# Shorter pieces for a softmax denominator, one key-shift row, and a new order of work on every engine

## The reference

```
x = x + linear_attention(group_norm(x))      # layer 0
x = x + conv(group_norm(x))                  # layer 1
```

## Time and profile before

| | |
|---|---|
| median of 3 runs | 1960.87 us (1960.73 to 1961.2) |
| time of the profiled execution | 1962.26 us |
| its span, first to last instruction | 1960.5 us |
| PE, DVE, ACT, POOL busy | 1861.5, 1632.6, 1369.6, 1311.3 us |
| DVE, ACT, POOL share of the span | 83%, 70%, 67% |
| mean granted PE clock | 0.989 |

### The profile page before, as it was taken

One profiled execution on the slowest core, in us unless ns is written; L12 is line 12 of the kernel. 1 busy time (PEld: TensorE's weight loads), 2 busy tenths in 40 slices (PEclk: granted clock), 3 DMA queues, 4 the chain that ended last, 5 costly groups with the idle time before them and its releaser, 6 DMA issues.

```text
span 1960.5 us, 51383 instructions
## 1 busy us (share of the span) xinstructions
PE 1861.5 (95%) x21521; PEld 993.2 (51%) x21521; DVE 1632.6 (83%) x3108; ACT 1369.6 (70%) x1480; POOL 1311.3 (67%) x729
## 2 busy tenths in 40 slices
PE   3799999999999999999999999999999999999997
PEld 1455554555554555544555544555544555544552
DVE  6778888888888788888888888888888888888874
ACT  4677776776776777766777766777676777766761
POOL 6476767686666676767676767676667686667670
PEclk8989999999999999999999999999999999999999
DMA  6267877887877797877788878787877797877765
GB/s 130 46 139 157 178 165 155 169 176 160 171 164 161 150 180 157 178 164 159 162 181 152 178 162 157 163 181 150 180 160 161 157 182 156 177 165 157 156 145 145
DMA packets 349430, 313.01 MB, mean 160 GB/s; under 512 B 299152, under 2 KB 299920, under 8 KB 341008
## 3 DMA queue, kind: packets, MB, share of 16 engines
q1 hardware_dynamic: 346656, 305.75, 75.3%
q10 hardware_dynamic: 2224, 3.97, 0.8%
q0 software_dynamic: 320, 0.01, 0.0%
HBM read 68.10 MB, written 67.11 MB: 69 GB/s over the span
## 4 chain that ended last, share of the span: by engine, by line
PE 54%; SPq 21%; DVE 18%; DMA 4%; issue 2%; ACT 1%; POOL 0%; ACTq 0%; DVEq 0%; POOLq 0%
PE pair_ps L922 18%; PE pair_ps L904 8%; DVE km L1286 7%; SPq L334 6%; SPq L321 5%; PE pair_ps L913 5%; PE pair_ps L863 4%; SPq L333 4%; DVE u L1283 4%; DVE image L1338 4%; PE pair_ps L885 3%; PE bank_ps L814 3%; DMA replicas<-yg_lo 3%; PE pair_ps L823 3%; SPq L306 2%; SPq L327 2%
## 5 line engine op out<-in xcount | busy, mean ns | idle before, releaser
L922 PE MATMUL pair_ps<-replicas,w_rep 96*32 96x512 f16 x8192 | 490.3, 383 | 18.0 <-DMA replicas<-yg_lo 18.0
L489 POOL TENSOR_TENSOR u_lo<-u,u_hi 128x1024 f16<-128x1024 f32 x128 | 269.9, 2139 | 280.2 <-ACT u_hi L608 280.2
L492 POOL TENSOR_TENSOR exp_kT_lo<-exp_kT,exp_kT_hi 128x1024 f16<-128x1024 f32 x128 | 273.1, 2134 | 192.8 <-ACT exp_kT_hi L620 190.2
L922 PEld LDWEIGHTS pair_ps<-replicas,w_rep 96*32 96x32 f16 x8192 | 201.6, 96 | 279.8 <-issue 76.7
L495 POOL TENSOR_TENSOR u_lo<-exp_q,u_hi 128x1024 f16<-128x1024 f32 x128 | 270.4, 2142 | 25.7 <-ACT u_hi L626 25.2
L608 ACT ACTIVATE u_hi<-u 128x1024 f16<-128x1024 f32 x128 | 135.3, 1057 | 144.5 <-DVE u L1283 137.5
L1338 DVE SCALAR_TENSOR_TENSOR image<-pair_ps,image 128x512 f32<-128x512 f32 x256 | 175.5, 686 | 45.3 <-PE pair_ps L922 41.3
L626 ACT ACTIVATE u_hi<-exp_q 128x1024 f16<-128x1024 f32 x128 | 131.5, 1050 | 109.2 <-DVE exp_q L1325 109.0
L485 POOL TENSOR_SCALAR u<-image,st 128x1024 f32<-128x1024 f32 x128 | 179.3, 1409 | 29.4 <-DVE st L1222 29.4
L863 PE MATMUL pair_ps<-wqk_hi,u_hi 128*128 128x128 f16 x1024 | 181.5, 222 | 0.0
L1325 DVE TENSOR_TENSOR exp_q<-exp_q,pair_ps 128x1024 f32<-128x1024 f32 x128 | 152.9, 1216 | 32.8 <-PE pair_ps L823 29.8
(11 more groups left out here) (184 smaller groups left out, 4500.2 us busy)
## 6 DMA issues: line engine op xcount, KB each, us to landing
image<-in_x SPq DMA_DIRECT2D x256, 256.0 KB, 4.8
out<-image SPq DMA_DIRECT2D x502, 128.0 KB, 2.3
replicas<-yg_hi SPq DMA_DIRECT2D x252, 165.0 KB, 3.7
replicas<-yg_hi SPq DMA_DIRECT2D x252, 107.2 KB, 2.4
replicas<-yg_lo SPq DMA_DIRECT2D x126, 165.0 KB, 4.2
replicas<-yg_lo SPq DMA_DIRECT2D x126, 107.2 KB, 2.3
uT_hi<-u_hi SPq DMA_TRANSPOSE x128, 4.4
uT_lo<-u_lo SPq DMA_TRANSPOSE x128, 4.0
```

Of the source, the lines that this page charges most:

```text
L489: pool.tensor_tensor(px(UL, v), px(U, v), px(UH, v), ALU.subtract).then_inc(ul_ready, 1)
L492: pool.tensor_tensor(KL[:, v % 2], KT[:, v % 2], KH[:, v % 2], ALU.subtract).then_inc(kl_ready, 1)
L922: mm = pe.matmul(conv_ps[32 * r:32 * r + 32, j % 2], w_rep[0:32 * SLOTS, tap, r], rep[:, j * ROWS + dy:(j + 1) * ROWS + dy, dx:dx + SIDE], ...
```

## The change

Three things.

- The reciprocal denominators of the queries are cut into two f16 pieces and no longer into three bf16 pieces. `den_parts` is one cast and one combining operation. The power on ACT carries a factor of 2^10 for this (`zcol[:, 2:3]`), which `spread_den`, a new f16 matrix made once in `split_conv_weights`, takes back. `den_broadcast` has a body of its own with the same number and size of matmuls. The norm's pieces stay three bf16.
- `krow` holds the row of key shifts once (33 x 128) and not four times (33 x 512); the matmul of `keys` reads it four times with a step of 0.
- The lists of all engines have another order. On PE: `inv_norm` 2 and `conv_ring` 5 come at the end of the step before; the rough keys alternate with `conv_ring` 6 and `conv_dense` 7; `rough_q` 0 comes ahead of `turn_k_max`, the y group means ahead of the keys; `keys` use pairs 1 and 2, `rough_q` 3 follows `keys` 3; the x group means come before `queries` 3, which comes after `context` 2; both first dense chunks precede `turn_context`; one ring chunk and a norm sum, and no longer two ring chunks, precede the first two denominator broadcasts; the last `mix` comes before `conv_dense` 4. On DVE: `normalise` 0 and 1 are at the end of the step before, ahead of `finish` 4; the four key maxima come nearly together; `y_moments` comes right behind `shift_k`, `y_seed` and `y_scale` among the query maxima; `soften` 3 comes ahead of `finish` 1. On ACT: `square_y` 0 and 1 follow `high_u` 0; `exp_memory` sits between `high_y` 0 and 1; `high_k` 2 precedes `exp_keys` 3; `high_y` 2 and 3 come earlier, before the first and the last `exp_queries`. SP's and POOL's lists are in the diff. In the drain ACT also issues the stores of units 0 and 1 of sample e.

The diff, cut; the lists of PE and DVE, and of ACT, beyond what stands here are told above:

```diff
-        krow = sb("krow", [33, 4, P], BF16)
+        krow = sb("krow", [33, P], BF16)
...
+        spread_den = sb("spread_den", [P, 2, P], F16)
...
                                  px(image(s), v)[32 * r:32 * r + 32]).then_inc(stored[v], 16)
 
             def step(p, a, c, e):
+                if e is not None:
+                    sp.wait_ge(out_ready, at(e, CHUNKS, 2))
+                    store(e, 0)
+                    sp.wait_ge(out_ready, at(e, CHUNKS, 4))
+                    store(e, 1)
                 if p is not None and p >= PRELOADED:
                     if e is not None:
                         sp.wait_ge(stored[0], at(e, 16 * RES, 16 * RES))
                     if e is not None:
                         sp.wait_ge(stored[1], at(e, 16 * RES, 16 * RES))
                     load(p, 0)
+                if a is not None:
+                    sp.wait_ge(ul_ready, at(a, UNITS, 1))
+                    turn_u(a, 0)
                 if e is not None:
                     sp.wait_ge(out_ready, at(e, CHUNKS, 6))
                     store(e, 2)
                 if a is not None:
-                    sp.wait_ge(ul_ready, at(a, UNITS, 1))
-                    turn_u(a, 0)
+                    sp.wait_ge(ul_ready, at(a, UNITS, 2))
+                    turn_u(a, 1)
                 if e is not None:
                     sp.wait_ge(out_ready, at(e, CHUNKS, 8))
                     store(e, 3)
                 if a is not None:
-                    sp.wait_ge(ul_ready, at(a, UNITS, 2))
-                    turn_u(a, 1)
+                    sp.wait_ge(ul_ready, at(a, UNITS, 3))
+                    turn_u(a, 2)
                 if p is not None and p >= PRELOADED:
                     if e is not None:
                         sp.wait_ge(stored[3], at(e, 16 * RES, 16 * RES))
@@ -390,8 +399,6 @@
                         sp.wait_ge(stored[2], at(e, 16 * RES, 16 * RES))
                     load(p, 1)
                 if a is not None:
-                    sp.wait_ge(ul_ready, at(a, UNITS, 3))
-                    turn_u(a, 2)
                     sp.wait_ge(ul_ready, at(a, UNITS, 4))
                     turn_u(a, 3)
...
@@ -519,34 +522,33 @@
                     pool.wait_ge(y_stat, at(c, Y_STEPS, Y_STEPS))
                     group_norm_y(c, 0)
                     group_norm_y(c, 1)
-                    if a is not None:
-                        pool.wait_ge(ul_ready, at(a, UNITS, 3))
-                    group_norm_y(c, 2)
                 if a is not None:
                     pool.wait_ge(kh_ready, at(a, UNITS, 3))
                     low_k(a, 2)
                 if c is not None:
-                    group_norm_y(c, 3)
                     pool.wait_ge(yg_ready, at(c, UNITS, 2))
                     pool.wait_ge(hi_ready, at(c, UNITS, 2))
                     low_y(c, 1)
+                    group_norm_y(c, 2)
                 if a is not None:
                     pool.wait_ge(kh_ready, at(a, UNITS, 4))
                     low_k(a, 3)
+                if c is not None:
+                    group_norm_y(c, 3)
                 if p is not None:
                     pool.wait_ge(x_stat, at(p, X_STEPS, X_STEPS))
                     group_norm_x(p, 0)
                     if c is not None:
                         pool.wait_ge(lo_odd, at(c, UNITS // 2, 1))
                     group_norm_x(p, 1)
+                    if c is not None:
+                        pool.wait_ge(lo_even, at(c, UNITS // 2, 2))
+                    group_norm_x(p, 2)
                 if c is not None:
                     pool.wait_ge(yg_ready, at(c, UNITS, 4))
                     pool.wait_ge(hi_ready, at(c, UNITS, 4))
                     low_y(c, 3)
                 if p is not None:
-                    if c is not None:
-                        pool.wait_ge(lo_even, at(c, UNITS // 2, 2))
-                    group_norm_x(p, 2)
                     if c is not None:
                         pool.wait_ge(lo_odd, at(c, UNITS // 2, 2))
                     group_norm_x(p, 3)
...
-                act.activation(den[:], den[:], ACT.Exp, scale=-1.0, bias=zcol[:, 0:1]).then_inc(den_act, 1)
+                act.activation(den[:], den[:], ACT.Exp, scale=-1.0, bias=zcol[:, 2:3]).then_inc(den_act, 1)
...
                     square_y(c, 2)
@@ -669,40 +675,44 @@
                     square_y(c, 3)
                 if a is not None:
                     act.wait_ge(kT_done, at(a, UNITS, 1))
-                    exp_keys(a, 0, pair_ps[2])
+                    exp_keys(a, 0, pair_ps[1])
                     act.wait_ge(kT_exp, at(a, UNITS, 1))
                     high_k(a, 0)
                     act.wait_ge(kT_done, at(a, UNITS, 2))
-                    exp_keys(a, 1, pair_ps[0])
+                    exp_keys(a, 1, pair_ps[2])
                     act.wait_ge(kT_exp, at(a, UNITS, 2))
                     high_k(a, 1)
                     act.wait_ge(kl_ready, at(a, UNITS, 1))
                     act.wait_ge(kT_done, at(a, UNITS, 3))
-                    exp_keys(a, 2, pair_ps[2])
+                    exp_keys(a, 2, pair_ps[1])
                 if c is not None:
                     act.wait_ge(y_stat, at(c, Y_STEPS, Y_STEPS))
                     high_y(c, 0)
+                if a is not None:
+                    exp_memory()
+                if c is not None:
                     high_y(c, 1)
                 if a is not None:
+                    act.wait_ge(ctx_sum, at(a, UNITS, 1))
+                    high_k(a, 2)
                     act.wait_ge(kl_ready, at(a, UNITS, 2))
-                    act.wait_ge(kT_done, at(a, UNITS, 4))
-                    exp_keys(a, 3, pair_ps[0])
-                    act.wait_ge(ctx_sum, at(a, UNITS, 1))
-                    act.wait_ge(kT_exp, at(a, UNITS, 3))
-                    high_k(a, 2)
+                    exp_keys(a, 3, pair_ps[2])
+                if c is not None:
+                    high_y(c, 2)
+                if a is not None:
                     act.wait_ge(q_done, at(a, UNITS, 1))
-                    exp_queries(a, 0, pair_ps[2])
+                    exp_queries(a, 0, pair_ps[1])
                     act.wait_ge(q_done, at(a, UNITS, 2))
-                    exp_queries(a, 1, pair_ps[1])
+                    exp_queries(a, 1, pair_ps[0])
                     act.wait_ge(kT_exp, at(a, UNITS, 4))
                     high_k(a, 3)
                     act.wait_ge(q_done, at(a, UNITS, 3))
-                    exp_queries(a, 2, pair_ps[0])
-                if c is not None:
-                    high_y(c, 2)
+                    exp_queries(a, 2, pair_ps[2])
+                if c is not None:
+                    high_y(c, 3)
                 if a is not None:
                     act.wait_ge(q_done, at(a, UNITS, 4))
-                    exp_queries(a, 3, pair_ps[1])
+                    exp_queries(a, 3, pair_ps[0])
                     act.wait_ge(den_sum, at(a, 1, 1))
                     den_log(bank_ps[1])
                     act.wait_ge(den_act, at(a, 2, 1))
@@ -710,9 +720,6 @@
                 if p is not None:
                     act.wait_ge(xg_ready, at(p, UNITS, 1))
                     square(p, 0)
-                if c is not None:
-                    high_y(c, 3)
-                if p is not None:
                     act.wait_ge(xg_ready, at(p, UNITS, 2))
                     square(p, 1)
...
             def den_broadcast(s, v, ps):
-                broadcast(ps, v, den_bcast)
+                if first(s) and v == 0:
+                    pe.wait_ge(setup_dve, SETUP_READY)
+                for j in (2 * v, 2 * v + 1):
+                    q = slice(32 * (j % 4), 32 * (j % 4) + 32)
+                    mm = pe.matmul(ps[:, (j % 2) * BANK:(j % 2 + 1) * BANK], spread_den[q, j // 4], parts[q].bitcast(F16),
+                                   start=True, stop=True, tile_position=(32 * (j % 4), 0))
+                mm.then_inc(den_bcast, 1)
...
-                    pe.matmul(ps[:, half * BANK:(half + 1) * BANK], ones_bf[q], krow[q].rearrange("p a b -> p (a b)"),
+                    pe.matmul(ps[:, half * BANK:(half + 1) * BANK], ones_bf[q], krow[q].unsqueeze(1).to_broadcast([1, 4, P]),
...
                     pe.wait_ge(mix_dve, at(a, 7, 2))
                     turn_context(bank_ps[1])
                 if c is not None:
-                    conv_dense(c, 1)
                     pe.wait_ge(lo_in[0], at(c, 16 * RES, 16 * RES))
                     pe.wait_ge(hi_in[0], at(c, 16 * 2 * RES, 16 * 2 * RES))
                     conv_ring(c, 0)
+                if p is not None:
+                    pe.wait_ge(sq_ready, at(p, UNITS, 1))
+                    norm_sums(p, 0, bank_ps[0])
+                if a is not None:
+                    pe.wait_ge(den_dve, at(a, 2, 2))
+                    den_broadcast(a, 0, pair_ps[0])
+                    den_broadcast(a, 1, pair_ps[1])
+                if c is not None:
                     conv_ring(c, 1)
-                if a is not None:
```

(22 more changed lines are left out.)

279 lines of the change are left out of this document (141 added, 138 removed).

## The result

The changed kernel takes 1991.6 us (median, 1990.3 to 1992.8), the kernel before 1961.0: a ratio of 1.0149 with a 95% interval of 1.0129 to 1.0169, so 31 us slower. The forecast was 1980, slower, with a range of 1930 to 2005. The profiled execution of after took 1990.32 us, its span is 1988.5.

What follows compares the result with a forecast made beforehand. PE was taken as the bound: floor 57.0 plus waits 1.0, DMA gap 0.1 and collision 1.3 gives period 59.4 against 58.8; some 30 periods add 18 us, setup 1, forecast 1980 us, range 1930 to 2005.

Steps and rivals of the forecast that it cites:

- forecast case: Whole kernel: period 59.4 against 58.8, time 1980 us; own case 1970 to 1992, chance 0.40.
- SyncE: SP queue, transposes issued earlier: replicas land 2.3 us earlier, ring's wait falls from 0.7 to 0.1, gain 0.6 a period.
- The collision: DVE's denominator combine waits for POOL's y subtract, takes 2.44 us, ends 10.4 us after G, the x group means' matmul.
- The gap it leaves on PE: Before the denominators' broadcast: PE waits 1.2 to 1.4 us a period for the late pieces, taken as 1.3.
- PE asks at G + 9.3: PE wants the denominators' pieces 9.3 us after the x group means' matmul, counting 0.5 for the moved norm sum.
- The layout: New PE and DVE order: four waits of 0.3, 0.3, 0.3 and 0.1 sum to 1.0 us a period, bounds 0.4 to 1.6.
- 57.0 is the floor of both kernels: PE's period without its four gaps: 57.0 us for both kernels, since no matmul is added or removed.
- Setup and drain: Setup: six small DVE operations under 1.5 us once, 1 us added; drain: zero, at most 4 us.
- Key-shift row once: DVE's key-shift copy falls from 0.41 to 0.2 us; step-0 operand costs at worst 1.6 us a period, taken as nothing.
- The signs: Denominators' combine median near 2.4 us, broadcast waits 1.3 every period, ring's replica wait nearly gone, DVE busier per period.
- The second collision: Rival: POOL's third key subtract precedes DVE's y unit 0 subtract; x group means 1.2 late, period 60.6, time 2016; chance 0.08.
- The undisturbed case: Rival: denominators' pieces meet no POOL work; period 58.1, time 1941, or 1929 with smaller gaps; chance 0.33.

Runs made afterwards that it cites:

- The PSUM experiment: Changed kernel with the denominators' cast and combining operation reading from a free PSUM bank: 1979.6 us, ratio to before 1.0085.
- the two kernels that have no collision: Changed kernel with POOL's group-norm subtractions of x half 2 waiting for the denominators' pieces, 1977.7 us; changed kernel with those pieces read from PSUM, 1979.6 us.
- both costs repaired: Changed kernel with denominators' pieces read from PSUM and norm 0's sums moved back behind ring 1: 1950.6 us, ratio to before 0.9942.
- pulling one pair apart: Changed kernel with PSUM pieces, sums together, setup in the preamble, plus rings 5 to 7 cut to fill PE's waits: 1944.9 us, ratio to before 0.9905.
- one move: Cut-ring kernel (with PSUM pieces, sums together, preamble setup), in the drain chunk 4's residual moved ahead of the y moments: 1941.1 us, 3.9 less.

## Why the prediction was right, and where it was right by luck

Sign, forecast case and even the period are as said: 59.4 forecast, 59.4 measured. The parts are not. From the medians of the runs: 1961.0, less 16 for SyncE's order, plus 29 for the split norm sums, 12 for the collision and 5.3 for the setup, is 1991.3 of 1991.6. The values belong to the order in which they were taken: SyncE's part is worth 28 in the new order.

- *The collision.* The mechanism held in each step: the cast waits a little (0.66 instead of 0.43), the subtract gets the turn, the combining takes 2.42. It ends at G + 10.43, forecast G + 10.4. By the Trainium skill's page "SBUF — State Buffer", section "Who interferes with whom", the shared ports are an exclusive lock and the loser waits for the whole instruction. The trace agrees more than I had read from the earlier trace rows: the combining ends 0.54 us after POOL's subtract, and the setup's 0.23 us operation ended 0.08 after the subtract beside it (67.23 + 2.35 against 67.63 + 2.03). The page also says that a DVE instruction with at most one input in SBUF, outside the modes that use both ports, does not contend with GpSimd. The PSUM experiment agrees: 0.75 us beside the same subtract. I cited the section and did not use this sentence, which held the repair.
- *The gap it leaves on PE.* Forecast 1.3, measured 0.49 a period. The failed term is "PE asks at G + 9.3": PE asks at G + 10.1 in the rows shown and at G + 10.0 in the other periods. I took 0.5 us for the moved norm sum, as half of the earlier trace rows; it took 0.96. And the denominators, behind queries 3 in the new order, took 2.26 us of slot against 1.86, as their last unit waits for ScalarE's exponential of those queries.
- *What stood in its place.* The same error, twice: the sum that was left behind also takes 0.95 and not 0.5. Together 0.85 us a period that no term of my sum held. 0.49 + 0.85 = 1.34 happens to be the 1.3 that I had put down for the collision. The number was right by compensation; without the collision I forecast 1941, and the two kernels that have no collision took 1977.7 and 1979.6.
- *The layout.* Forecast 1.0 us of waits above a floor of 57.0. With both costs repaired the period is 58.05: right again, and again by compensation. The failed step is "57.0 is the floor of both kernels, as no matmul is added or removed". The new order puts six of the eight broadcasts in pairs of units, which take 0.33 us for two where each unit alone takes 0.32 (the third measured by pulling one pair apart, above): three times 0.31 is the 0.93 that the table has beside the old wait. Against it stand longer waits than the listed ones, by the table: dense convolutions 0.83 (the waits ahead of the first and the fourth rough keys, forecast 0.6), denominators 0.40 (not forecast), turns 0.38 (0.33 in the other periods).
- *SyncE.* A gain of 0.6 forecast, 0.63 measured (58.77 to 58.15 on average). The reason was right, its size not quite: the replicas are issued 1.4 us earlier in after than in before (9.6 against 11.0), not 2.3.
- *Setup and drain.* "1 us" was 5.3. The step that failed: under 1.5 us for the operations (five and not six; 4.0 beside POOL, 3.0 even in the preamble), and "DVE works on the first sample then" was taken as cover, when the x statistics behind it were what PE waited for next. The drain's zero to 4 was 2.3 by the table, and one move took 3.9.
- *Key-shift row once.* 0.2 us for the copy forecast, 0.22 measured; the window holds no longer matmuls of the keys. No gain or loss of its own was isolated.
- *The signs.* The combining operation's median and the rings' wait came as said. Two signs did not: the broadcast waits 0.49 us and not 1.3, and DVE is not busier, 49.97 us a period against 50.14, although its combining takes 1.7 longer. Its two low parts of y take 2.44 us together and took 3.06 before, which offsets that; why was not looked into.
- *Rivals.* The second collision did not come: DVE's subtract was first and POOL's key subtract took 3.16 us instead of 2.13, once a period, off PE's path. The undisturbed case had the largest single chance of the faster ones, 0.33, and its time of 1941 could not have come true with the sums split.

## What to carry to other kernels

When matmuls that use a part of TensorE's rows or columns are moved, price them by their neighbours and not by a share of the row that they stood in: apart they take the full slot, and the busy share doesn't tell. Before filling a wait of PE with a cut piece of a group, subtract what the cut costs, here 0.11 to 0.16 us for a ring. And where a VectorE operation meets GpSimd, look first at its inputs: one of them in a free PSUM bank did about as much as making GpSimd wait (12 and 14 us).

## What the hardware showed that was not expected

- Two units of norm sums, in the timeline 4 matmuls of 32 columns each: 0.96 us back to back for both, 0.95 to 0.96 for one alone. Two broadcasts from different groups of 32 rows: 0.33 together, 0.32 each alone.
- A ring of 32 matmuls of 32 columns takes 1.86 us whole; cut once by full-width matmuls 1.97 to 2.02.
- A DVE operation of 0.23 us on 128x256 f16, one input in SBUF, took 2.03 us beside a POOL subtract: having only one input in SBUF doesn't free an operation from the wait. The combining with one input in SBUF and one in PSUM was free of it 32 times out of 32.
- With nothing in its way, the pipeline repeats to 0.02 us: after's steady periods lie between 59.38 and 59.40. Scatter from period to period was here a sign of a DMA on the path.
